# Attention inside a macaron block: one scores pass a round with masks and maxima on VectorE, and probabilities turned by DMA

## The chip, the cores and the metric

The kernel runs on one core of a Trainium2 chip. The metric is the device time of one execution in microseconds. The kernel before took 1144.59 us, the median of three runs (1144.28 to 1146.37).

## The reference

A macaron block on x of shape (8, 256, 256): half a mixture-of-experts FFN, attention, and the same FFN again, each behind a layernorm. Inputs and output are float32.

```python
x = x + 0.5 * ffn(layernorm(x), router_w, gate_w, up_w, down_w)
x = x + attn(layernorm(x), Wq, bq, Wk, bk, Wv, bv, Wo, bo, q_gain)
x = x + 0.5 * ffn(layernorm(x), router_w, gate_w, up_w, down_w)

def attn(x, ...):                      # 16 query heads, 4 key/value heads, head width 16
    q, k, v = x @ Wq.T + bq, x @ Wk.T + bk, x @ Wv.T + bv
    q, k = rope(rms_norm(q)), rope(rms_norm(k))
    q = q * q_gain
    s = where(causal, (q * 16 ** -0.5) @ k.T, -inf)       # 256 x 256 for each head
    return softmax(s) @ v @ Wo.T + bo

def ffn(x, ...):                       # 8 experts, width 512, router weights kept to top-p 0.9
    w = top_p(softmax(x @ router_w.T), 0.9)
    return sum_e w[:, e] * ((silu(x @ gate_w[e].T) * (x @ up_w[e].T)) @ down_w[e].T)
```

## The kernel before

The 2048 tokens lie in 16 tiles of 128, and four tiles are a block. All experts run on all tokens. The FFN work is 64 units (`UNITS`: which FFN, which block, which expert) of four groups each, 256 groups in all. A group is six matmuls of 512 columns into G, six into U (L339, `pe_gu`) and, some slots later, twelve of 256 columns into YB (L358, `pe_y`); products are made of float16 high and low parts, which is why there are so many.

Everything is ordered by hand in slots 0 to 512. `pe_slot`, `act_slot`, `dve_slot`, `pool_slot` and `sp_slot` say what each engine issues in a slot. In an even slot TensorE issues the gate and up matmuls of a group, in an odd slot the down matmuls of an older group, and behind these whatever attention work is due there. Nothing ties an engine to a slot but the order of its own instructions and its waits on semaphores (the lanes in `L`). ScalarE takes the tanh of G (L553) and the high half of the product (L560), VectorE the two products (L685, L690) and the sum into X (L706), GpSimd the low half (L1061). This FFN work runs throughout, for the first FFN and then the second, and attention is threaded between it from about slot 104 to 440.

A batch is two tiles (256 tokens), one even and one odd, and takes 36 slots. Its attention work is:

- `pe_qkv` (L423) makes q, k and v of a tile into S2. VectorE and GpSimd norm and rotate them (the power by -0.5 on GpSimd is L1117). ScalarE (`act_qh`) and VectorE (`dve_ql`) write high and low parts into QS and KS, and SP turns these by transposing DMAs into QKT (`sp_qt`, `sp_kt`).
- The first scores pass, `pe_max` (L443 for even tiles, L449 for odd ones), has queries on partitions and keys along the free axis, into banks S0 and S1: a head pair of 64 contraction rows each, by `tile_position`. VectorE (`dve_max`, L930) adds the mask and takes each row's maximum; `dve_mm` writes it in two parts into spare columns of QS, and `sp_q2` turns the whole of QS a second time.
- The second scores pass, `pe_scores` (L469), runs once for each of 32 items (batch, key/value head), every nine slots. It has keys on partitions and queries along the free axis, in three banks, and the maxima enter the product through the spare rows. ScalarE raises it (`act_exp`, L626), GpSimd zeroes what lies above the diagonal (`pool_mask`, L1149), ScalarE makes the high half (`act_ph`, L634) and GpSimd the low half (`pool_pl`, L1157) in `room`. `pe_pv` (L492) multiplies by v seven slots behind the scores, and VectorE scales the result (`dve_pv`). In this layout the probabilities are already turned as `pe_pv` needs them.
- `pe_op_tp` (L501) and `pe_op_mm` (L507) project the output of a tile, which is added to X.

S2 is shared by `pe_qkv`, `pe_pv`, the output projection and the later routers. A TensorE wait in the middle of this order delays all FFN work behind it.

Of the kernel before, what the change touches and what calls it, by code (L numbers as in the profile page):

```python
# [27 lines left out]
NI = 2 * NT  # L28
# [7 lines left out]
MASKED = -128.0  # L36
# [16 lines left out]
PER = 9  # L53
BATCH = 4 * PER
FIRST = 138
ITEM = [FIRST + PER * i for i in range(NI)]

def by_tile(name):

    first, second, even, odd = AT[name]
    slots = [first, second]
    for t in range(2, NT, 2):
        slots += [FIRST + BATCH * (t // 2 - 2) + even, FIRST + BATCH * (t // 2 - 2) + odd]
    return slots

AT = {'at': (108, 114, 16, 33), 'qkv': (110, 116, 21, 39), 'qt': (117, 123, 28, 46), 'kt': (117, 123, 28, 46), 'q2': (125, 135, 45, 69)}
MAX0 = (120, 122, 126, 128, 130, 132)
MAXB = (38, 41, 50, 56, 59, 66)
OUT = (5, 15)
FTP0 = (3, 3, 6, 6)
FIRST_FTP = (99, 102, 104, 109, 152, 152, 161, 161)
FTP_LATER, ROUTE_LATER = (22, 25)
ROUTE_FIRST = (3, 11, 112, 162)
# [45 lines left out]
def build(nc, d):  # L124
    with ExitStack() as ctx:
# [53 lines left out]
        GM, GE, GR, ESC = (sb(c, [P, 1], F32) for c in ('GM', 'GE', 'GR', 'ESC'))  # L179
# [3 lines left out]
        MB = sb('MB', [P, 2, P], F16)  # L183
# [13 lines left out]
        QS = sb('QS', [P, 2, H, 4, HD], F16)  # L197
# [3 lines left out]
        MXN = sb('MXN', [P, KVH, G // 2, 2], F32)  # L201
        RC = sb('RC', [P, 2 * G], F32)
        RD = sb('RD', [P, 2 * G, HD], F32)
        OB = sb('OB', [P, 2, 2, KVH, G * HD], F32)
# [11 lines left out]
        s_qt, s_q2 = ([sem(f's_{c}{i}') for i in range(2)] for c in ('qt', 'q2'))  # L216
        s_kt = sem('s_kt')
# [4 lines left out]
        for name, labels in [  # L222
# [4 lines left out]
                ('v_fst', 'stats'), ('v_fag', 'aggr'), ('v_fep', 'eps'), ('v_fx', 'xn'), ('v_ls', 'ls mx sub'), ('v_rp', 'sum rc p eq gt'), ('v_wt', 'cum wt'), ('v_wb', 'wtc'), ('v_wc', 'wc'),  # L227
                ('v_al', 'stats aggr eps'), ('v_ax', 'xn'), ('v_qb', 'qb'), ('v_ss', 'ss ms'), ('v_rb', 'rb1 rb0 r'), ('v_qn', 'qn'), ('v_ql', 'qlo klo'), ('v_mp', 'a b'), ('v_mm', 'm1 m2'), ('v_pv', 'rc rd ob'), ('v_op', 'ad'),
                ('g_lo', 'lo'), ('g_w', 'lo2'), ('g_frs', 'rs'), ('g_fl', 'xl'), ('g_rk', 'eq b bp'), ('g_ars', 'rs'), ('g_al', 'xl'), ('g_bo', 'bo'), ('g_sq', 'sq'), ('g_rr', 'rr sg'), ('g_qz', 'z'), ('g_ra', 'ra'), ('g_v', 'v1 r1 v2 r2 v3'), ('g_mk', 'a c'), ('g_pl', 'b a c'), ('g_rw', 'b1 r1 b2 r2 b3')]:
# [62 lines left out]
        def s0_read(eng, s):  # L292
            eng.wait_ge(*L['a_e'].at(before(ITEM, s), 'a'))
            eng.wait_ge(*L['v_mp'].at(before(MAXS, s), 'a'))
# [17 lines left out]
        def s2_read(eng, s):  # L312
            eng.wait_ge(*L['a_e'].at(before(ITEM, s), 'c'))
# [5 lines left out]
            pv_read(eng, s, (3,))  # L319
            if before(ROUTE, s) >= 3:  # L320
                eng.wait_ge(*L['v_ls'].at(before(ROUTE, s), 'ls'))

        def pv_read(eng, s, places):
            i = max((i for i in range(NI) if i % 4 in places and ITEM[i] + I_STEP['pv'] < s), default=-1)
            eng.wait_ge(*L['v_pv'].at(i, 'rd'))
# [79 lines left out]
        def pe_atp(eng, t, s):  # L405
            s1_read(eng, s)
            eng.wait_ge(*L['a_ax'].at(t, 'xh'))
            eng.wait_ge(*L['g_al'].at(t, 'xl'))
            for q in range(2 * KD):
                mm = eng.transpose(S1[:, :].bitcast(F16)[:, q * P:(q + 1) * P], XA16[:, q // KD, q % KD * P:(q % KD + 1) * P], ident16[:, :])  # L410
            mm.then_inc(L['p_at'].sem, 1)

        def pe_qkv(eng, t, s):
# [3 lines left out]
            if t < 2:  # L417
                eng.wait_ge(*L['a_ac'].at(t, 'xt'))
# [8 lines left out]
        def pe_max(eng, n, s):  # L427
            t, j = MAXP[n]
# [4 lines left out]
            if t == 0:  # L433
                eng.wait_ge(s_i2, 3)
            keys = QKT[:, t // 2 % 2, :, H // 2:, :]
            qk = QKT[:, t // 2 % 2, :, :, :]
            rows = lambda h: slice(64 * h, 64 * h + 64)
            if t % 2 == 0:

                for q in range(4):  # L440
                    kv = 2 * j + q // 2
                    for h, bank in ((0, S0), (1, S1)):
                        mm = eng.matmul(bank[:, q * P:(q + 1) * P], qk[rows(h), t % 2, 2 * kv + q % 2, :], keys[rows(h), 0, kv, :], start=q == 0, stop=q == 3, skip_group_check=True, tile_position=(64 * h, 0))  # L443
                        if q == 3:
                            mm.then_inc(L['p_mx'].sem, 1)
# [1008 lines left out]
```

## Time and profile before

| what | value |
|---|---|
| median of three runs | 1144.59 us |
| the profiled execution | 1144.43 us |
| its span, first to last instruction | 1142.2 us |
| TensorE matmuls (PE) | 1112.3 us busy, 97% |
| VectorE (DVE) | 809.9 us busy, 71% |
| GpSimd (POOL) | 668.2 us busy, 59% |
| ScalarE (ACT) | 518.2 us busy, 45% |
| the transposing and loading DMA queue | 11.4% of 16 engines |

Busy time is the time in which an engine had an instruction in work. Matmuls overlap one another, so a group's cost to the span is best read from the starts of its neighbours in the timeline, not from durations. "Idle before" is how long the engine stood idle ahead of a group, and the releaser is what ended that.

### The profile page before, as it was taken

Reading aid. Unit: us, or ns where it says so; the run is one execution under the profiler, and the core shown is the slowest. Engines: PE = TensorE matmul, PEld = TensorE weight load, DVE = VectorE, ACT = ScalarE, POOL = GpSimd, SP = SyncE. Lnnn points to the kernel's source line nnn. Section 1 sums busy time; section 2 is a strip of 40 time slices with the busy share of each in tenths; the row PEclk is TensorE's granted clock in tenths of the full one; section 3 lists DMA queues with packets and bytes.
Section 4 is the critical chain, followed back from the end, with each engine's and each line's share of the span. In section 5 each row is a group of like instructions: output and inputs, shape, how many; then the busy total and the mean of one; then the engine's idle time right before and its main releaser. Section 6 shows DMA issues by size and latency. Waiting matters only on the chain.

```text
span 1142.2 us, 21578 instructions
## 1 busy us (share of the span) xinstructions
PE 1112.3 (97%) x7689; PEld 660.5 (58%) x7689; DVE 809.9 (71%) x1993; ACT 518.2 (45%) x868; POOL 668.2 (59%) x737
## 2 busy tenths in 40 slices
PE   5899999999999999999999999999999999999998
PEld 2456556565555555565565655555656566665665
DVE  7878887679788777778777778768767455554443
ACT  4544544433454554445445454454454544333332
POOL 4545444368488677667767768768655464333222
PEclk9999999999999999999999999999999999999999
DMA  5411110001110110011111011021110000000000
GB/s 185 133 56 56 63 62 2 9 11 42 29 33 15 29 29 19 19 29 24 16 29 24 15 29 24 16 46 25 25 24 20 10 11 1 11 19 1 1 1 20
DMA packets 73273, 34.66 MB, mean 30 GB/s; under 512 B 65360, under 2 KB 69968, under 8 KB 73168
## 3 DMA queue, kind: packets, MB, share of 16 engines
q1 hardware_dynamic: 73168, 33.27, 11.4%
q8 instruction: 64, 1.05, 0.4%
q14 instruction: 41, 0.34, 0.1%
HBM read 15.70 MB, written 2.10 MB: 16 GB/s over the span
## 4 chain that ended last, share of the span: by engine, by line
PE 63%; DVE 5%; POOL 4%; issue 1%; ACT 1%; DVEq 0%; ACTq 0%; POOLq 0%
PE YB L358 19%; PE G L339 19%; PE U L339 18%; PE S L492 1%; PE S L469 1%; PE S L507 1%; DVE S L930 1%; PE S L423 1%; POOL HS L1061 1%; POOL room L1157 1%; DVE TS L685 1%; DVE TS L690 1%; POOL RR L1117 1%; PE S L449 1%; DVE X L706 1%
## 5 line engine op out<-in xcount | busy, mean ns | idle before, releaser
L1061 POOL TENSOR_TENSOR HS<-TS,HS 128x512 f16<-128x512 f32 x256 | 301.1, 1176 | 379.4 <-ACT HS L560 378.4
L358 PE MATMUL YB<-W,HS 128*128 128x256 f16 x3036 | 374.4, 273 | 9.7 <-DVE X L706 6.3
L339 PE MATMUL G<-XS,W 128*128 128x512 f16 x1536 | 375.0, 380 | 1.7 <-ACT XS L585 1.7
L339 PE MATMUL U<-XS,W 128*128 128x512 f16 x1536 | 373.5, 379 | 1.1 <-DVE W L791 1.1
L358 PEld LDWEIGHTS YB<-W,HS 128*128 128x128 f16 x3036 | 290.0, 98 | 92.3 <-DVE X L706 13.4
L685 DVE SCALAR_TENSOR_TENSOR TS<-TS,G 128x512 f32<-128x512 f32 x256 | 175.3, 685 | 223.3 <-ACT TS L553 223.1
L560 ACT ACTIVATE HS<-TS 128x512 f16<-128x512 f32 x256 | 161.4, 631 | 311.7 <-DVE TS L690 311.5
L553 ACT ACTIVATE TS<-G,TSC 128x512 f32<-128x512 f32 x256 | 175.5, 686 | 216.5 <-PE G L339 210.2
L339 PEld LDWEIGHTS U<-XS,W 128*128 128x128 f16 x1536 | 150.3, 98 | 182.9 <-DVE W L791 1.6
L339 PEld LDWEIGHTS G<-XS,W 128*128 128x128 f16 x1536 | 146.9, 98 | 135.3 <-issue 2.0
L690 DVE SCALAR_TENSOR_TENSOR TS<-TS,U 128x512 f32<-128x512 f32 x256 | 176.0, 688 | 28.7 <-DVE TS L685 1.8
L706 DVE SCALAR_TENSOR_TENSOR X<-YB,WTC,X 128x256 f32<-128x256 f32 x253 | 121.9, 482 | 56.0 <-PE YB L358 53.9
L1157 POOL TENSOR_TENSOR room<-room 128x512 f16<-128x512 f32 x96 | 109.9, 1160 | 2.8 <-ACT room L634 2.8
L930 DVE CUSTOM_DVE_ANT_0 S<-S,MB 128x128 f32<-128x128 f32 (+1 forms) x256 | 82.7, 391 | 0.0
L626 ACT ACTIVATE room<-S,ESC 128x512 f32<-128x512 f32 x96 | 62.3, 682 | 16.1 <-PE S L469 15.8
L634 ACT ACTIVATE room<-room 128x512 f16<-128x512 f32 x96 | 59.6, 621 | 17.9 <-POOL room L1149 16.9
L1117 POOL TENSOR_TENSOR RR<-MS,MH 128x20 f32<-128x20 f32 x16 | 56.6, 3540 | 0.2
L1149 POOL TENSOR_SCALAR_AFFINE_SELECT room<-room 128x512 f32<-128x512 f32 x64 | 40.7, 642 | 0.5 <-ACT room L626 0.5
L1070 POOL TENSOR_TENSOR RSF<-VEF,MH 128x1 f32<-128x1 f32 x24 | 14.4, 600 | 42.5 <-DVE VEF L813 42.5
L930 DVE DVE_READ_ACCUMULATOR2_ANT MXN<- 128x1 f32 x256 | 36.3, 142 | 0.0
L492 PEld LDWEIGHTS S<-VS,room 128*128 128x128 f16 x768 | 24.0, 96 | 4.1
L492 PE MATMUL S<-VS,room 128*128 128x49 bf16 x768 | 24.5, 184 | 0.0
(167 smaller groups left out, 712.5 us busy)
## 6 DMA issues: line engine op xcount, KB each, us to landing
room<-in_gate SPq DMA_DIRECT2D x4, 512.0 KB, 3.2
room<-in_up SPq DMA_DIRECT2D x4, 512.0 KB, 3.2
room<-in_down SPq DMA_DIRECT2D x4, 512.0 KB, 3.6
QKT<-in_gate SPq DMA_DIRECT2D x4, 512.0 KB, 3.3
QKT<-in_up SPq DMA_DIRECT2D x4, 512.0 KB, 3.6
QKT<-in_down SPq DMA_DIRECT2D x4, 512.0 KB, 4.5
out_y<-X SPq DMA_DIRECT2D x16, 128.0 KB, 1.8
X<-in_x SPq DMA_DIRECT2D x3, 512.0 KB, 6.2
```

Of the source, the lines that this page charges most:

```text
L339: mm = eng.matmul(bank[:, :], W[:, e, wl, jj, kk * I + m * P:kk * I + (m + 1) * P], flat(XS16[:, b % 2, xl, kk, :, :], 'cq'), start=q == 0 ...
L358: mm = eng.matmul(out, HS[:, j % 2, hl, kk, m * P:(m + 1) * P], W[:, e, wl, 2, kk * D:(kk + 1) * D], start=kk + hl + wl == 0, stop=kk == K ...
L553: eng.activation(TS[:, k % 3, :], GB[k % 2][:, :], ACT.Tanh, scale=TSC[:, e, :]).then_inc(L['a_t'].sem, 1)
L560: eng.activation(HS[:, j % 2, 0, m, :], TS[:, k % 3, :], ACT.Copy).then_inc(L['a_h'].sem, 1)
L626: eng.activation(flat(P32[:, blk, :, :], 'gk'), bank[:, :], ACT.Exp, scale=ESC[:, 0:1]).then_inc(L['a_e'].sem, 1)
L685: eng.scalar_tensor_tensor(TS[:, k % 3, :], TS[:, k % 3, :], 1.0, GB[k % 2][:, :], ALU.add, ALU.mult).then_inc(L['v_t'].sem, 1)
L690: eng.scalar_tensor_tensor(TS[:, k % 3, :], TS[:, k % 3, :], H_C, UB[k % 2][:, :], ALU.mult, ALU.mult).then_inc(L['v_h'].sem, 1)
L706: eng.scalar_tensor_tensor(x, y, WTC[:, b, m, e:e + 1], x, ALU.mult, ALU.add).then_inc(L['v_y'].sem, 1)
L930: mx = eng.tensor_tensor_reduce(x, x, mask, -1.0, 3.0e38, ALU.add, ALU.min, out)
L1061: eng.tensor_tensor(HS[:, j % 2, 1, m, :], TS[:, k % 3, :], HS[:, j % 2, 0, m, :], ALU.subtract).then_inc(L['g_lo'].sem, 1)
L1117: eng.tensor_tensor(RR[:, :], MS[:, :], MH[:, :], ALU.pow).then_inc(L['g_rr'].sem, 1)
L1157: eng.tensor_tensor(flat(PL[:, blk, :, :], 'gk'), flat(P32[:, blk, :, :], 'gk'), flat(PH[:, blk, :, :], 'gk'), ALU.subtract).then_inc(L['g ...
```

## The change

The second scores pass goes, and with it the second turning of QS. There is one pass a round, in the layout of the old `pe_max`, and 48 rounds in place of 32 items: two for each even tile (8 heads each, keys of one tile) and four for each odd tile (4 heads, keys of two tiles), every six slots from slot 128. In a round TensorE fills S0 and S1 (L411 of the new program). VectorE masks, scales by the negative scale and takes the minimum: for even tiles one masking instruction over the bank and one reduction, for odd tiles the old combined instruction twice. ScalarE raises each head by an instruction of its own, with the row's minimum as bias, then makes the high half; GpSimd makes the low half. GpSimd's masking goes. Since probabilities now have queries on partitions, one transposing DMA a round turns high and low parts of both banks (2048 columns, sixteen 128x128 blocks) into QKT or PT1 (`sp_pt`). TensorE waits for that DMA before `pe_pv`, eight slots behind the scores. The transposes of the first two tiles' XA move from TensorE to a DMA. Slots of the projections, the output and the second FFN's normalization shift accordingly.

```diff
-PER = 9
-BATCH = 4 * PER
-FIRST = 138
-ITEM = [FIRST + PER * i for i in range(NI)]
+PER = 6
+BATCH = 6 * PER
+FIRST = 126
+ROUND = [FIRST + 2 + PER * i for i in range(NR)]
+ROUNDS = [(2 * b + (r > 1), r - 2 if r > 1 else r) for b in range(B) for r in range(6)]
...
-Q_STEP = {'rb1': 2, 'sq': 2, 'rb0': 2, 'rr': 3, 'r': 4, 'qn': 5, 'qz': 4, 'v': 5, 'qh': 6, 'ql': 6}
-I_STEP = {'eb': 1, 'ea': 1, 'ma': 2, 'ec': 2, 'hb': 3, 'mc': 3, 'ha': 4, 'lb': 4, 'hc': 5, 'la': 4, 'lc': 5, 'pv': 7, 'o': 8}
+Q_STEP = {'rb1': 2, 'sq': 2, 'rb0': 2, 'rr': 3, 'r': 4, 'qn': 5, 'v': 5, 'qh': 6, 'ql': 6, 't': 7}
+I_STEP = {'ma': 1, 'mb': 2, 'ea': 2, 'eb': 3, 'ha': 3, 'hb': 4, 'la': 4, 'lb': 5, 't': 6, 'pv': 8, 'o': 9}
...
+ATP, QKVP, OUTP = (by_tile(-17, -5), by_tile(-12, 0), by_tile(18, 42))
...
-        def pe_max(eng, n, s):
...
+        def pe_scores(eng, i, s):
+            t, j = ROUNDS[i]
+            s0_read(eng, s)
+            s1_read(eng, s)
+            q_turned(eng, t)
+            k_turned(eng, t)
...
+            heads, keys = (4, 1) if t % 2 == 0 else (2, 2)
+            for q in range(heads):
+                kv, c = (2 * j + q // 2, 4 * j + q) if t % 2 == 0 else (j, 2 * j + q)
+                for h, bank in ((0, S0), (1, S1)):
+                    mm = eng.matmul(bank[:, q * keys * P:(q + 1) * keys * P], QTT[rows(h), t % 2, c, :], KTT[rows(h), t // 2 % 2, 0:keys, kv, :], start=q == 0, stop=q == heads - 1, skip_group_check=True, tile_position=(64 * h, 0))
...
-            part(S2, 1, (1,), 0).then_inc(L['p_s0'].sem, 1)
-            part(S1, 0, (0, 1), 1).then_inc(lane.sem, 1)
-            part(S0, 0, (0, 1), 0).then_inc(lane.sem, 1)
...
+        def pe_pv(eng, i, s):
+            t, j = ROUNDS[i]
             s2_read(eng, s)
+            eng.wait_ge(*L['g_v'].at(t, 'v3'))
+            p_turned(eng, i)
...
+                            mm = eng.matmul(o, PT[i % 2][:, h, hl * G + q * keys + kt, :], VS[:, t // 2 % 3, kt, kv, :], start=kt + hl == 0, stop=kt == keys - 1 and hl == 1)
...
+            for q in range(heads):
+                a = eng.activation(P32[:, h, q * width:(q + 1) * width], (S0, S1)[h][:, q * width:(q + 1) * width], ACT.Exp, bias=MXN[:, i % 2, h, q:q + 1], scale=-1.0)
+            a.then_inc(L['a_e'].sem, 1)
...
+            if t % 2 == 0:
+                x = bank[:, :].rearrange('p (g k) -> p g k', g=G)
+                eng.scalar_tensor_tensor(x, x, NESC[:, 0:1], MB[:, 1, :].unsqueeze(1).broadcast_to([P, G, P]), ALU.mult, ALU.subtract).then_inc(lane.sem, 1)
+                eng.wait_ge(*lane.at(i, 'x' + 'ab'[h]))
+                eng.tensor_reduce(MXN[:, i % 2, h, :], x, AX.X, ALU.min).then_inc(lane.sem, 1)
+            else:
+                for q in range(2):
+                    x = bank[:, q * 2 * P:(q + 1) * 2 * P]
+                    eng.tensor_tensor_reduce(x, x, flat(MB[:, :, :], 'ak'), NESC[:, 0:1], 3.0e38, ALU.add, ALU.min, MXN[:, i % 2, h, q:q + 1]).then_inc(lane.sem, 1)
...
-        def pool_mask(eng, i, c):
...
+        def pool_pl(eng, i, h):
+            eng.wait_ge(*L['a_ph'].at(i, 'ab'[h]))
+            eng.tensor_tensor(PHL[:, i % 2, h, 1, :], P32[:, h, :], PHL[:, i % 2, h, 0, :], ALU.subtract).then_inc(L['g_pl'].sem, 1)
...
-        def sp_q2(eng, t):
...
+        def sp_pt(eng, i):
...
+                eng.wait_ge(*L['p_pv'].at(i - 2, 'pv'))
+            eng.wait_ge(*L['a_ph'].at(i, 'b'))
+            eng.wait_ge(*L['g_pl'].at(i, 'b'))
+            eng.dma_start(PT[i % 2].rearrange('p h c q -> p (h c) q'), flat(PHL[:, i % 2, :, :, :], 'hsk'), transpose=True).then_inc(s_pt[i % 2], 16)
```

TensorE's order in the middle of the attention, before: G, U and YB are the FFN's matmuls, S<-VS,room is `pe_pv`, S<-WO,OT the output projection, and S<-QKT the scores, by L469 in the second pass and by L449 in the first.

```order
L358 MATMUL YB<-W,HS 128x256 x12
L469 MATMUL S<-QKT 128x256
L469 MATMUL S<-QKT 128x512 x2
L469 MATMUL S<-QKT 128x256
L339 MATMUL G<-XS,W 128x512 x6
L339 MATMUL U<-XS,W 128x512 x6
...
L449 MATMUL S<-QKT 128x256 x4
L358 MATMUL YB<-W,HS 128x256 x12
...
L492 MATMUL S<-VS,room 128x49 x24
```

The same engine in the changed kernel, one round of an even tile with the next round's scores: L411 is the scores, L428 `pe_pv` of the round before, from PT1 or QKT.

```order
L411 MATMUL S<-QKT 128x128 x8
L338 MATMUL YB<-W,HS 128x256 x12
...
L428 MATMUL S<-VS,PT 128x49 x16
L338 MATMUL YB<-W,HS 128x256 x12
...
L436 MATMUL S<-ident,OB 128x128 x2
...
L411 MATMUL S<-QKT 128x128 x8
L442 MATMUL S<-WO,OT 128x256 x2
...
L428 MATMUL S<-VS,QKT 128x49 x16
```

The groups of L469 are gone and nothing of their shape has come in; the product with v is in groups of 16 matmuls where it was in groups of 24.

SP's order in one batch before: the last two letters of a name tell what is turned, QS the queries (by L1252 the first time, by L1261 with the maxima), KS the keys, XA the normed tile for the projections.

```order
L1252 DMA_TRANSPOSE QKT<-QS 128x8x128
L1257 DMA_TRANSPOSE QKT<-KS 128x4x128
L1261 DMA_TRANSPOSE QKT<-QS 128x8x128
L1238 DMA_TRANSPOSE XTA<-XA 128x4x128
L1261 DMA_TRANSPOSE QKT<-QS 128x8x128
```

And in the changed kernel, where `room` holds the probabilities (L1164 is `sp_pt`); XS<-XF is for the second FFN.

```order
L1128 DMA_TRANSPOSE XS<-XF 128x4x128 x2
L1134 DMA_TRANSPOSE XTA<-XA 128x4x128
L1147 DMA_TRANSPOSE QKT<-QS 128x8x128
L1155 DMA_TRANSPOSE QKT<-KS 128x4x128
L1164 DMA_TRANSPOSE QKT<-room 128x16x128
L1164 DMA_TRANSPOSE PT<-room 128x16x128
L1147 DMA_TRANSPOSE QKT<-QS 128x8x128
L1155 DMA_TRANSPOSE QKT<-KS 128x4x128
```

The two turnings with maxima have left the queue, and six turnings of sixteen blocks a batch have come in; once a batch one of them stands directly behind those of XA, QS and KS.

## Rows read from the trace of the kernel before

**Rows 1.** The page: busy time and share of the span by engine, then TensorE's granted clock.
```profile
PE 1112.3 (97%) x7689; PEld 660.5 (58%) x7689; DVE 809.9 (71%) x1993; ACT 518.2 (45%) x868; POOL 668.2 (59%) x737
PEclk9999999999999999999999999999999999999999
```

**Rows 2.** Waits of TensorE: us in total, times, longest.
```profile
PE YB L358 <- DVE X L706: 6.3, 8, 1.7
PE YB L358 <- POOL HS L1061: 3.2, 5, 1.9
```

**Rows 3.** The second scores pass among TensorE's groups: busy us, mean ns | idle before.
```profile
L469 PE MATMUL S<-QKT 64*128 64x256 f16 (+1 forms) x128 | 19.8, 330 | 0.0
```

**Rows 4.** TensorE's timeline in the middle of the attention: start us, duration us.
```profile
588.82 1.46 PE L339 MATMUL U<-XS,W 128*128 128x512 f16 x6
590.21 0.39 PE L449 MATMUL S<-QKT 64*128 64x256 f16 x4
590.53 1.49 PE L358 MATMUL YB<-W,HS 128*128 128x256 f16 x12
...
594.66 0.76 PE L492 MATMUL S<-VS,room 128*128 128x49 bf16 x24
595.27 1.47 PE L358 MATMUL YB<-W,HS 128*128 128x256 f16 x12
...
597.44 1.46 PE L339 MATMUL G<-XS,W 128*128 128x512 f16 x6
598.74 1.46 PE L339 MATMUL U<-XS,W 128*128 128x512 f16 x6
600.12 0.62 PE L469 MATMUL S<-QKT 64*128 64x256 f16 x4
600.68 1.48 PE L358 MATMUL YB<-W,HS 128*128 128x256 f16 x12
602.00 1.46 PE L339 MATMUL G<-XS,W 128*128 128x512 f16 x6
```

**Rows 5.** Groups of VectorE, by shape.
```profile
L690 DVE SCALAR_TENSOR_TENSOR TS<-TS,U 128x512 f32<-128x512 f32 x256 | 176.0, 688 | 28.7 <-DVE TS L685 1.8 <-PE G L339 0.5
L948 DVE TENSOR_REDUCE RD<-S 128x128 f32<-128x384 f32 x32 | 16.2, 507 | 0.0
```

**Rows 6.** Groups of ScalarE, by shape.
```profile
L626 ACT ACTIVATE room<-S,ESC 128x512 f32<-128x512 f32 x96 | 62.3, 682 | 16.1 <-PE S L469 15.8
L639 ACT ACTIVATE OT<-S 128x256 f32<-128x256 f32 x16 | 6.0, 376 | 0.0
```

**Rows 7.** Groups of GpSimd, by shape.
```profile
L1061 POOL TENSOR_TENSOR HS<-TS,HS 128x512 f16<-128x512 f32 x256 | 301.1, 1176 | 379.4 <-ACT HS L560 378.4
L1157 POOL TENSOR_TENSOR room<-room 128x512 f16<-128x512 f32 x96 | 109.9, 1160 | 2.8 <-ACT room L634 2.8
L1117 POOL TENSOR_TENSOR RR<-MS,MH 128x20 f32<-128x20 f32 x16 | 56.6, 3540 | 0.2
L1149 POOL TENSOR_SCALAR_AFFINE_SELECT room<-room 128x512 f32<-128x512 f32 x64 | 40.7, 642 | 0.5 <-ACT room L626 0.5
L1112 POOL TENSOR_TENSOR RA<-QKV,COS 128x320 f32<-128x320 f32 x16 | 14.9, 931 | 0.0
```

**Rows 8.** GpSimd's timeline: the first and last of the five instructions of `pool_v`.
```profile
619.07 0.50 POOL L1136 CAST VS<-QKV 128x64 bf16<-128x64 f32 x1
...
620.71 0.24 POOL L1144 CAST VS<-VR 128x64 bf16<-128x64 f32 x1
```

**Rows 9.** DMA issues: count, median us from issue to landing.
```profile
QKT<-QS SPq DMA_TRANSPOSE x32, 2.8
XS<-XF SPq DMA_TRANSPOSE x24, 2.4
```

**Rows 10.** SP's timeline: two turnings issued back to back.
```profile
579.58 1.23 SPq L1252 DMA_TRANSPOSE QKT<-QS  x1
...
580.91 1.22 SPq L1257 DMA_TRANSPOSE QKT<-KS  x1
```

More of the change, by code:

```diff
@@ L52, with by_tile, last_round @@
 PREP = [-99, 0, 8, 24, 36, 47, 58, 72, 83]
-PER = 9
-BATCH = 4 * PER
-FIRST = 138
-ITEM = [FIRST + PER * i for i in range(NI)]
[L61 to L74, printed above, removed]
+PER = 6
[3 more added lines that the diff above has]
+ROUNDS = [(2 * b + (r > 1), r - 2 if r > 1 else r) for b in range(B) for r in range(6)]
+def by_tile(even, odd):
+    return [FIRST + BATCH * (t // 2) + (odd if t % 2 else even) for t in range(NT)]
+def last_round(t):
+    return 6 * (t // 2) + (5 if t % 2 else 1)
 FTP0 = (3, 3, 6, 6)
 FIRST_FTP = (99, 102, 104, 109, 152, 152, 161, 161)
-FTP_LATER, ROUTE_LATER = (22, 25)
-ROUTE_FIRST = (3, 11, 112, 162)
+FTP_SOON, FTP_LATER, FTP_LAST, ROUTE_LATER = ((66, 68), (62, 64), (30, 51), 67)
+ROUTE_FIRST = (3, 11, 112, 174)
 A_STEP = {'ax': 3, 'xl': 3, 'bo': 6}
-Q_STEP = {'rb1': 2, 'sq': 2, 'rb0': 2, 'rr': 3, 'r': 4, 'qn': 5, 'qz': 4, 'v': 5, 'qh': 6, 'ql': 6}
-I_STEP = {'eb': 1, 'ea': 1, 'ma': 2, 'ec': 2, 'hb': 3, 'mc': 3, 'ha': 4, 'lb': 4, 'hc': 5, 'la': 4, 'lc': 5, 'pv': 7, 'o': 8}
+Q_STEP = {'rb1': 2, 'sq': 2, 'rb0': 2, 'rr': 3, 'r': 4, 'qn': 5, 'v': 5, 'qh': 6, 'ql': 6, 't': 7}
+I_STEP = {'ma': 1, 'mb': 2, 'ea': 2, 'eb': 3, 'ha': 3, 'hb': 4, 'la': 4, 'lb': 5, 't': 6, 'pv': 8, 'o': 9}
 R_STEP = {'r1': 1, 'ex': 1, 'r2': 1, 'r2b': 3, 'rank': 3, 'r3': 5}
@@ L215, in build @@
         s_ft, s_at = ([sem(f's_ft{i}') for i in range(2)], sem('s_at'))
-        s_qt, s_q2 = ([sem(f's_{c}{i}') for i in range(2)] for c in ('qt', 'q2'))
-        s_kt = sem('s_kt')
+        s_qt, s_kt = (sem('s_qt'), sem('s_kt'))
+        s_pt = [sem(f's_pt{i}') for i in range(2)]
         N_AW = 8
@@ L403, in pe_ftp @@
             mm.then_inc(L['p_ft'].sem, 1)
[L405 to L411, printed above, removed]
         def pe_qkv(eng, t, s):
@@ L434, in pe_max @@
                 eng.wait_ge(s_i2, 3)
-            keys = QKT[:, t // 2 % 2, :, H // 2:, :]
-            qk = QKT[:, t // 2 % 2, :, :, :]
             rows = lambda h: slice(64 * h, 64 * h + 64)
[L438 to L445, printed above, removed]
-            else:
-                for q in range(2):
-                    for h, bank in ((0, S0), (1, S1)):
-                        mm = eng.matmul(bank[:, q * 2 * P:(q + 1) * 2 * P], qk[rows(h), t % 2, 2 * j + q, :], keys[rows(h), :, j, :], start=q == 0, stop=q == 1, skip_group_check=True, tile_position=(64 * h, 0))
-                        if q == 1:
-                            mm.then_inc(L['p_mx'].sem, 1)
@@ L477, in pe_pv @@
-        def pe_pv(eng, i, s):
-            bank = (S0, S0, S1, S2)[i % 4]
-            (s0_read, s0_read, s1_read, s2_read)[i % 4](eng, s)
-            b, kv = divmod(i, 4)
-            eng.wait_ge(*L['g_v'].at(2 * b + 1, 'v3'))
-            eng.wait_ge(*L['a_ph'].at(i, 'c'))
-            eng.wait_ge(*L['g_pl'].at(i, 'c'))
-            for qt in range(2):
-                for g in range(G):
-                    o = bank[:, (qt * G + g) * VW:(qt * G + g + 1) * VW]
-                    terms = [(g % 2, 2 * qt + g // 2, 0)] + [(2, 2 * (g % 2) + g // 2, 1)] * qt
-                    q = 0
-                    for blk, at, kt in terms:
-                        for ph in (PH, PL):
-                            mm = eng.matmul(o, ph[:, blk, at, :], VS[:, b % 3, kt, kv, :], start=q == 0, stop=q == 2 * len(terms) - 1)
-                            q += 1
+            heads, keys = (4, 1) if t % 2 == 0 else (2, 2)
@@ L1269, in sp_slot @@
+        def sp_slot(eng, s):
+            for i in due(ROUND, s, I_STEP['t']):
+                sp_pt(eng, i)
+            for t in due(ATP, s):
+                sp_atp(eng, t)
+            for t in due(QKVP, s, Q_STEP['t']):
                 sp_qt(eng, t)
-            for t in due(KTP, s):
                 sp_kt(eng, t)
```

286 lines of the change are left out of this document (108 added, 178 removed), and 4 rows, old and new, of the table later.

## The prediction

> **What bounds the kernel now.** I read the page first: TensorE has matmuls in work for 1112.3 of 1142.2 us, no other engine is above 71%, and the granted clock is at its full level (2.4 GHz) in all 40 slices [rows 1]. Then its waits: of those that fall in the steady part the two largest, for VectorE's sum into X and for GpSimd's low half, are 6.3 and 3.2 us together over the whole span [rows 2]. So TensorE is the bound, and the question for each edit is what it does to the stream of matmuls. Durations mislead there, since matmuls overlap; I read the stream by starts [rows 4]. G to U is 1.30 us, YB to the next G 1.32, so a gate, up and down group, two slots, is 3.92 us. Whatever stands between two such starts beyond that is attention's cost on TensorE.
>
> **What goes from TensorE.** The second scores pass: 32 calls of four matmuls. U at 598.74 should be followed by the next group at 600.04; with the call between them YB starts at 600.68, so the call costs 0.64 us, 0.08 of it ahead of its first matmul [rows 4]. The merged busy time of the group, 19.8 us over 32 calls, is 0.62 each, which is the same thing with its tail overlapping what follows [rows 3]. I take 0.65 us: 32 x 0.65 = 20.8 us go. As these stand in the stream of the engine that is the bound, they come off the end in full if nothing new is waited for. The eight small transposes of the first two tiles go too; I leave them out.
>
> At this place a rule can be weighed. The row first: the call streams 2x256 and 2x512 = 1536 columns, with 64 contraction rows in each half of the array. Six full-height matmuls of 512 columns take 1.30 us, 0.42 ns a column, so 1536 columns one after another would be 0.65 us. The call costs 0.64 us [rows 4], so the two halves gain next to nothing here. The Trainium skill (TensorEngine Tiling (Array Packing)) says of contraction dimensions up to 64 that two row tiles work at once, for up to twice the speed. By that the call would be worth 0.32 us and the change 10.4 us instead of 20.8; the trace does not agree.
>
> **What stays the same on TensorE.** The 48 scores calls have the shapes of the old first pass: 16 of eight 128-column matmuls, 32 of four 256-column ones. The old call costs 590.53 - 588.82 - 1.30 = 0.41 us [rows 4], before and after. The product with v is 768 matmuls in both, in 48 calls of 16 for 32 of 24. A call of 24 costs 595.27 - 594.66 = 0.61 us, 25 ns a matmul [rows 4]. If all of that is per matmul, 16 more calls cost nothing; if each has a lead-in like the scores call's 0.09 us (590.21 - 588.82 - 1.30), they cost 1.4 us. I take 0.7.
>
> **The new wait.** TensorE waits for a sixteen-block turning before each `pe_pv`, and all FFN work stands behind it. The trace has no turning of that size. Eight blocks (QS) land 2.8 us after issue, four (XS) 2.4 [rows 9]; a straight line gives 0.1 us a block and 3.6 us for sixteen. From below it is not faster than the four-block one, 2.4; from above twice the eight-block one, 5.6. I take 3.6, as the two rows lie so close together that most of it is fixed. By the Trainium skill (DMA: Bandwidth & Descriptors, on the effective rate of a DMA transpose with a non-contiguous middle dimension, 261 GB/s) the 524 KB would move in an estimated 2.0 us, eight blocks more than QS costing 1.0 and the landing being 3.8; no row here shows that rate by itself.
>
> Is there time for it? Count from the end of a round's scores on TensorE, 0. The matmuls with v come four groups later, with one scores call and one call with v between: 4 x 3.92 + 0.4 + 0.4 = 16.5 us. On the other side:
> - VectorE ends the product with U at about 0.5 and then has an even tile's mask (as L690, 0.69) and the reduction over 512 (L948 has 384 in 0.51, so 0.68) [rows 5]: first bank 1.9. The second bank follows the next sum into X, about 3.8.
> - ScalarE: 256 elements are 376 ns, 512 are 682, so 1.2 ns an element and some 0.22 us for 128, 0.9 us for four heads [rows 6]. Second bank raised by 4.9. S0 and S1 are free then, and the next scores come at 3 x 3.92 + 0.4 = 12.2. That wait is hidden by 7 us.
> - GpSimd has a low half of the FFN at 6.1 to 7.3 (its input comes that late), then the two low halves of the probabilities, 1.16 each [rows 7]: 9.6.
> - The turning is issued at 9.7 and lands at 13.3. Slack 3.2 us.
>
> The tight round is the one in which the next even tile is projected, once a batch for seven batches. GpSimd has squares and rotation (L1112, 0.93) before 0, then the power, 3.54, which can start at about -0.3 and with its small follower ends at 3.6; an FFN low half, 4.8 [rows 7]; the five instructions for v, 620.95 - 619.07 = 1.9 [rows 8], 6.7; another FFN half, 7.9; the low half of the other tile's XA, half the size of L1061, 0.6: 8.5; and the two halves of the probabilities, 10.8. SP has XA, QS and KS ahead of the probabilities in its queue, at 1.33 us from issue to issue [rows 10]: 8.5 + 4.0 = 12.5. Landing at 16.1 against 16.5. The starting points in these two lists are my estimates from the order and these durations, good to about 1 us, so some of the seven rounds will wait: from 0 (all early) to 1.6 us each (the 5.6 landing: 12.5 + 5.6 - 16.5). I take 0.2, 1.4 us in all.
>
> **Other engines.** GpSimd loses 64 maskings of 0.64 us [rows 7] and keeps 96 low halves, in a stream that is off the bound. VectorE keeps the odd tiles' 256-wide instructions, has 0.69 + 0.68 a bank for the even tiles and loses the writing of maxima. ScalarE raises in 256 smaller instructions instead of 96: 128 x 0.22 + 128 x 0.38 = 77 us where it had 96 x 0.68 = 65. It is 45% busy [rows 1], and the tanh it owes TensorE stands behind 0.9 us of this in a slot where it stood behind two of 0.68, so nothing. The lighter VectorE and GpSimd can give back part of the 9.5 us of [rows 2]; bounds 0 and -9.5, and since VectorE's bursts (both banks' maxima in one slot) are spread over two, I take -2.5.
>
> **The sum.** Against the profiled execution's own 1144.43 us (span 1142.2; the median of the runs is 1144.59, the same within 0.2 us): -20.8 + 0.7 + 1.4 - 2.5 = -21.2, which gives 1123.2 us, say 1123.
>
> **Rivals.**
> - A: the tight rounds stall. If sixteen blocks take 5.6 us, seven rounds wait 1.6 us: 11.2 in place of 1.4, 1133. For it: three turnings directly ahead in the queue. Against: the small step from four to eight blocks.
> - B: the bound passes for moments to VectorE or GpSimd in the projection rounds, where the power and both scores' work now meet in six slots instead of nine. At 0.5 us in each of the 16 projection rounds, and nothing given back, that is 8 + 2.5 = 10.5 us more: 1133.7. Against: both engines lose work.
> - C: the second pass was partly hidden, as the rule on row tiles has it, and is worth 10.4 us: 1133.6. Against it the gap in [rows 4].
> - D, slower: the turning becomes the pace of every round. Slack of an ordinary round is 16.5 - 9.7 - landing. With a landing above 6.8 each of 48 rounds waits, and the 21 us are gone at 0.44 us a round, a landing of 7.25. At 8.0: 48 x 1.2 = 58 us, 1181. For it: the probabilities are the longest turning in the kernel, and everything hangs on it. Against: it needs almost three times the eight-block landing.
>
> **How the numbers follow.** A difference of 0.2% (2.3 us) is about what a measurement can tell. Forecast 0.66, between 1118 (all of [rows 2] given back, no stall) and 1128; A 0.14; B 0.08; C 0.04; D 0.05; something between D and A that ends within 0.2% of before 0.03. Faster: 0.66 + 0.14 + 0.08 + 0.04 = 0.92; same 0.03; slower 0.05. The range holds the forecast, A, B and C: 1117 to 1135.
>
> **What the profile after would show.** No group of four matmuls with 512 columns; the scores calls still at 0.41 us and calls with v at 0.40 to 0.49 by starts; TensorE's span less idle down by about 20 us. Sixteen-block turnings landing in 3.6 us. In TensorE's waits, S<-VS waiting for a DMA or its turned probabilities would appear seven times and briefly; many times, or by more than 1 us, is A or D. YB waiting for VectorE or GpSimd for more than the 9.5 us of now is B. A gain near 10 with no such waits is C. The prediction is wrong if the time is above 1135, and its reasoning is wrong if the scores calls have become dearer or the turning lands after 5 us.

## The result, and the profile after

The changed kernel takes 1158.99 us (median; 1156.32 to 1160.62) where the one before, timed beside it, takes 1144.69: a ratio of 1.012 (95% interval 1.0097 to 1.0143). Forecast were 1123.0 us and a range from 1117 to 1135. The change makes the kernel 14 us slower, and the prediction was wrong in sign.

The page of the kernel after, first busy time and share by engine, then TensorE's granted clock in 40 slices:

```profile
PE 1098.6 (95%) x7553; PEld 658.0 (57%) x7553; DVE 834.8 (72%) x1817; ACT 544.0 (47%) x1026; POOL 629.5 (54%) x657
PEclk9999999999999999999999999999999999999999
```

Against [rows 1] TensorE has 13.7 us less in work and its span is 14.2 us longer (1156.4 for 1142.2): the idle time grew by 28 us. No other engine has become the bound. Its waits, in us, times and longest:

```profile
PE YB L338 <- DVE X L627: 16.9, 16, 2.7
PE S L428 <- DMA QKT<-room: 16.3, 8, 3.6
PE YB L338 <- POOL HS L976: 3.8, 5, 0.9
PE S L428 <- DMA PT<-room: 0.7, 1, 0.7
```

Two things stand there that [rows 2] did not have. The product with v (L428) waits for the turning in QKT eight times, in all 16.3 us: once 0.2 us in the first round, and between 1.1 and 3.6 us in each of the seven rounds in which the next even tile is projected, the tight ones of the prediction; and the wait of YB for VectorE's sum into X has gone from 6.3 to 16.9 us. The group of the second pass [rows 3] is gone; what attention has left there is, as line, tile and shape, count, then busy us and mean ns:

```profile
L411 PE MATMUL S<-QKT 64*128 64x128 f16 (+1 forms) x256 | 18.9, 246 | 0.0
L428 PE MATMUL S<-VS,PT 128*128 128x49 bf16 x384 | 13.6, 184 | 0.7 <-DMA PT<-room 0.7
```

Taken by starts, as the prediction did it, one can sum up how much later than usual each group of matmuls starts, given what stands ahead of it. After the first 255 us this excess over the calls' own cost is 7.8 us before and 43.3 after: +35.5. The 32 gaps of the removed pass sum to 20.9. +35.5 - 20.9 = +14.6, against the 14.2 us by which the spans differ. So the account closes with two entries: **the saving came in full, and 35 us of new waits, and of what follows from them, came with it.**

The turnings (count, median us from issue to landing), which answer to [rows 9]:

```profile
QKT<-room SPq DMA_TRANSPOSE x24, 4.3
PT<-room SPq DMA_TRANSPOSE x24, 4.3
QKT<-QS SPq DMA_TRANSPOSE x16, 2.8
QKT<-KS SPq DMA_TRANSPOSE x16, 2.4
```

**A round that waits.** The timeline after, all engines mixed (start us, duration us, engine; in brackets the idle time before and what ended it). It is the tight round of the prediction; its scores end at 684.16.

```profile
683.67 0.32 DVE L812 TENSOR_SCALAR MS<-SS 128x20 f32<-128x20 f32 x1
683.77 0.39 PE L411 MATMUL S<-QKT 64*128 64x256 f16 x4
...
685.70 0.49 DVE L856 CUSTOM_DVE_ANT_0 S<-S,MB,NESC 128x256 f32<-128x256 f32 x1
686.10 0.42 DVE L786 BATCH_NORM_STATS2 STA<-X 128x6 f32<-128x256 f32 x1
...
686.77 0.15 DVE L790 TENSOR_SCALAR VEA<-MVA 128x1 f32<-128x1 f32 x1
...
687.01 0.55 POOL L1003 TENSOR_TENSOR RSA<-VEA,MH 128x1 f32<-128x1 f32 x1 [2.42 <-DVE VEA L790]
...
687.52 3.54 POOL L1032 TENSOR_TENSOR RR<-MS,MH 128x20 f32<-128x20 f32 x1
...
688.43 0.48 DVE L822 TENSOR_TENSOR RA<-RA,RB 128x320 f32<-128x320 f32 x1
...
693.27 1.48 PE L338 MATMUL YB<-W,HS 128*128 128x256 f16 x12 [0.81 <-DVE X L627]
...
696.11 2.27 POOL L1058 TENSOR_TENSOR room<-room 128x512 f16<-128x512 f32 x2
696.24 1.19 SPq L1134 DMA_TRANSPOSE XTA<-XA  x1
...
697.52 1.26 SPq L1147 DMA_TRANSPOSE QKT<-QS  x1
...
698.87 1.22 SPq L1155 DMA_TRANSPOSE QKT<-KS  x1
...
700.20 1.79 SPq L1164 DMA_TRANSPOSE QKT<-room  x1
700.62 1.46 PE L319 MATMUL U<-XS,W 128*128 128x512 f16 x6
...
704.59 0.56 PE L428 MATMUL S<-VS,QKT 128*128 128x49 bf16 x16 [2.52 <-DMA QKT<-room]
```

The power's input MS is there at 683.99, as forecast. But ahead of the power GpSimd has `pool_a_rs` (L1003), the statistic of the odd tile, due in the same slot, and that waits for `dve_a_stats`, which stands in VectorE's order behind the first maxima (L856). GpSimd is idle for 2.42 us and works 0.55 on it; the power starts at +3.4 us where the prediction has -0.3. Everything behind it is late by as much: the low halves of the probabilities end at 698.38, +14.2 (forecast 10.8), and the turning is issued at 700.20, +16.0 (forecast 12.5), behind the three turnings that the prediction counted. It lands 4.3 us later, not 3.6. The product could have started at 701.9. The same wait over the whole span, first after, then before:

```profile
POOL RSA L1003 <- DVE VEA L790: 45.5, 15, 3.6
```
```profile
POOL RSA L1088 <- DVE VEA L869: 13.3, 4, 4.8
```

Eight of the fifteen waits after stand directly ahead of a power, 20.8 us in all; behind the other seven none follows. Two things hang on the late power in this order: the low halves of the probabilities, and the low half of XA (L1007), behind which XA, QS and KS are turned ahead of the probabilities. The halves are ready at +14.2, so 1.8 us of the +16.0 are the queue of SP.

### The profile page after: what moved, and what is told of

Its sections match the earlier page's. It is cut to its first block, busy times and chain, and to the rows that moved or that the text cites. A ratio compares the mean times of both kernels' runs of the same rounds, so it can differ in the third digit from the quotient of the medians.

```text
span 1156.4 us, 21016 instructions
## 1 busy us (share of the span) xinstructions
PE 1098.6 (95%) x7553; PEld 658.0 (57%) x7553; DVE 834.8 (72%) x1817; ACT 544.0 (47%) x1026; POOL 629.5 (54%) x657
## 4 chain that ended last, share of the span: by engine, by line
PE 55%; POOL 8%; issue 3%; DMA 3%; DVE 2%; SPq 1%; ACT 1%; DVEq 0%; POOLq 0%; ACTq 0%
PE YB L338 18%; PE G L319 16%; PE U L319 16%; DMA QKT<-room 3%; POOL RR L1032 2%; POOL HS L976 2%; PE S L442 1%; PE S L428 1%; POOL room L1058 1%; PE S L411 1%; SPq L1155 1%; POOL XF L989 1%; PE S L393 1%; POOL RA L1027 1%; DVE X L627 1%
## 5 line engine op out<-in xcount | busy, mean ns | idle before, releaser
L338 PE MATMUL YB<-W,HS 128*128 128x256 f16 x3036 | 377.3, 274 | 20.8 <-DVE X L627 16.9
L319 PEld LDWEIGHTS G<-XS,W 128*128 128x128 f16 x1536 | 150.0, 98 | 130.8 <-issue 2.6
L551 ACT ACTIVATE room<-S,MXN 128x128 f32<-128x128 f32 (+1 forms) x256 | 90.3, 420 | 28.2 <-DVE MXN L852 15.3
L856 DVE CUSTOM_DVE_ANT_0 S<-S,MB,NESC 128x256 f32<-128x256 f32 x128 | 56.9, 486 | 0.0
L1003 POOL TENSOR_TENSOR RSA<-VEA,MH 128x1 f32<-128x1 f32 x16 | 8.9, 558 | 45.5 <-DVE VEA L790 45.5
L428 PE MATMUL S<-VS,QKT 128*128 128x49 bf16 x384 | 13.7, 184 | 16.3 <-DMA QKT<-room 16.3
L428 PEld LDWEIGHTS S<-VS,QKT 128*128 128x128 f16 x384 | 12.7, 96 | 23.8 <-issue 20.0
L850 DVE SCALAR_TENSOR_TENSOR S<-S,NESC,MB 128x512 f32<-128x512 f32 x32 | 24.0, 751 | 0.0
```

The lines of the kernel that those rows point to most:

```text
L319: mm = eng.matmul(bank[:, :], W[:, e, wl, jj, kk * I + m * P:kk * I + (m + 1) * P], flat(XS16[:, b % 2, xl, kk, :, :], 'cq'), start=q == 0 ...
L338: mm = eng.matmul(out, HS[:, j % 2, hl, kk, m * P:(m + 1) * P], W[:, e, wl, 2, kk * D:(kk + 1) * D], start=kk + hl + wl == 0, stop=kk == K ...
L551: a = eng.activation(P32[:, h, q * width:(q + 1) * width], (S0, S1)[h][:, q * width:(q + 1) * width], ACT.Exp, bias=MXN[:, i % 2, h, q:q + ...
```

## The experiments

Each kernel was timed in three rounds beside the one before (about 1144.3 us there). W is the theory that the place of the odd tile's statistics decides: GpSimd waits for VectorE there, ahead of the power, and the turning is late. Q is its rival, that the turnings' own size and their queue decide, so that an earlier power gives little. All edits but e5's start from the changed kernel.

**e1: the odd tile's norm two slots earlier,** so that its statistics leave the slot of the power.

```diff
-ATP, QKVP, OUTP = (by_tile(-17, -5), by_tile(-12, 0), by_tile(18, 42))
+ATP, QKVP, OUTP = (by_tile(-17, -7), by_tile(-12, 0), by_tile(18, 42))
```

> From the changed kernel (1159.0), the whole normalization of odd tiles, its turning included, two slots earlier. Theory W (wait in front of the power): the changed kernel loses its gain because GpSimd waits in its order for the odd tile's statistics ahead of the 3.5 us power, which then runs 3 to 4 us late and makes the turning of the probabilities, TensorE's wait for it and the late sums into X; so TensorE's waits for turned probabilities fall from 17 us to under 2, those for sums into X from 17 to about 6, the clock stays at full, and the time is 1122 to 1130. Theory Q (queue and size of the turning): the turning is late because it stands behind three others and lands in 4.3 us instead of 3.6; only XA leaves its front, 1.3 of the 2.5 us of each of eight rounds go, and the time is 1146 to 1150.

Measured: 1139.79 us, ratio 0.996 (0.9946 to 0.9975). That is 19.2 us below the changed kernel, by one number in a table. TensorE's waits:

```profile
PE YB L338 <- DVE X L627: 13.6, 24, 2.0
PE S L428 <- DMA QKT<-room: 2.8, 3, 1.6
PE S L428 <- DMA PT<-room: 1.3, 2, 0.7
```

Those for the turning fall from 17.0 to 4.1 us, where W had them under 2, and neither range holds the time: W expected 1122 to 1130, Q 1146 to 1150, and 13.6 us of waits for the sum into X stay where W had about 6. The place of the odd tile's norm matters, and it is not the only cause.

**e2: the odd tile's norm without its turning, two slots earlier.** All that goes by `ATT` moves: the statistics, GpSimd's power for them, and the high and low half of XA. Only the slot in which SP issues the turning of XA stays.

```diff
-ATT = [s - 4 for s in ATP]
+ATT = [s - 4 - 2 * (t % 2) for t, s in enumerate(ATP)]
```

> From the changed kernel, only the statistics and the split of odd tiles two slots earlier; the turning of XA keeps its place behind which the others stand in the queue. Theory W: 1122 to 1132, as the power starts 3 us earlier and all behind it moves. Theory Q: nothing has left the queue, the time stays above 1154.

Measured: 1140.09 us, ratio 0.9963 (0.9948 to 0.9977). The same tight round in e2:

```profile
668.68 0.70 POOL L1003 TENSOR_TENSOR RSA<-VEA,MH 128x1 f32<-128x1 f32 x1 [1.40 <-DVE VEA L790]
...
671.04 0.39 PE L411 MATMUL S<-QKT 64*128 64x256 f16 x4
...
673.92 3.53 POOL L1032 TENSOR_TENSOR RR<-MS,MH 128x20 f32<-128x20 f32 x1
...
679.58 1.19 SPq L1134 DMA_TRANSPOSE XTA<-XA  x1
...
682.38 2.27 POOL L1058 TENSOR_TENSOR room<-room 128x512 f16<-128x512 f32 x2
...
684.75 1.76 SPq L1164 DMA_TRANSPOSE QKT<-room  x1
...
689.16 0.56 PE L428 MATMUL S<-VS,QKT 128*128 128x49 bf16 x16
```

The scores end at 671.43, the turning is issued at +13.3 (it was +16.0), and the product waits for nothing. The edit is worth 18.9 us. The time misses both ranges (W 1122 to 1132, Q above 1154), and the rows show that the edit did not part the two theories. The power starts at +2.5, only 0.9 us earlier than in the changed kernel: GpSimd now waits 1.40 us and works 0.70 for the same statistic ahead of the squares and the rotation, which start 2.1 us later for it. XA is turned at +8.2 where it was +12.1, since its low half no longer stands behind the five instructions for v; so the three turnings are out of the way, and the probabilities go out 0.1 us after their low halves (684.65). Of the 2.7 us, about 1.0 come from GpSimd's earlier halves and 1.7 from the queue. The same holds for e1, where XA is turned at +8.2 in this round too.

**e3: the turning one slot earlier,** ahead of the three others in SP's queue.

```diff
-... 'lb': 5, 't': 6, 'pv': 8, 'o': 9}
+... 'lb': 5, 't': 5, 'pv': 8, 'o': 9}
```

> From the changed kernel, the probabilities' turning is put ahead of XA, QS and KS in the queue, one slot earlier. Theory W: the two low halves are ready 1.8 us before the turning is issued, so at most 1.8 of the 2.5 us of eight rounds go, perhaps with some clock, while the late sums into X stay: 1138 to 1146. Theory Q: all of the wait goes and the sums with it, 1122 to 1130.

Measured: 1143.45 us, ratio 0.9992 (0.9982 to 1.0002), 15.5 us better than the changed kernel; waits for the turning 5.4 us in seven and 0.7 in one, where they were 17.0, those for the sum still 16.9. It lies in W's range (1138 to 1146), not in Q's (1122 to 1130). The power is as late as before (+3.4); the turning goes out at +14.3, right behind the low halves, and the granted clock falls once where it fell three times. The late power and the queue are links of one chain. Taking the queue away alone gives 15.5 us; no run makes the power alone earlier, so its share is not measured by itself.

**e4: the product with v one slot later,** with all that follows it.

```diff
-... 't': 6, 'pv': 8, 'o': 9}
-ATP, QKVP, OUTP = (by_tile(-17, -5), by_tile(-12, 0), by_tile(18, 42))
+... 't': 6, 'pv': 9, 'o': 10}
+ATP, QKVP, OUTP = (by_tile(-17, -5), by_tile(-12, 0), by_tile(19, 43))
```

> From the changed kernel (1159.0), the product with v and its scaling one slot later, the output projection one slot later behind it; GpSimd's order and the queue are untouched. Theory W (the power runs late behind the wait for statistics, and the turning and the sums into X are late with it): the turning is still late, by 2.5 us of which the later place hides 1.3, in eight rounds 10 us, with 3 to 5 us of clock; the late sums into X stay at about 17 us: 1143 to 1148. If instead the turning were the only late thing, the rest of its wait would be small and the time near 1135.

Measured: 1152.83 us, ratio 1.0078 (1.0063 to 1.0093): a miss, 5 us above the expected 1143 to 1148. Waits of TensorE, then two groups and two rows of VectorE and one of GpSimd:

```profile
PE YB L338 <- DVE X L627: 22.6, 22, 2.6
PE S L428 <- DMA QKT<-room: 6.9, 6, 2.0
```
```profile
L869 DVE TENSOR_TENSOR OB<-RD,RC 128x64 f32<-128x64 f32 x32 | 22.4, 700 | 1.1
L869 DVE TENSOR_TENSOR OB<-RD,RC 128x128 f32<-128x128 f32 x16 | 16.1, 1004 | 0.6
```
```profile
574.07 1.08 DVE L869 TENSOR_TENSOR OB<-RD,RC 128x128 f32<-128x128 f32 x1
575.41 0.69 DVE L606 SCALAR_TENSOR_TENSOR TS<-TS,G 128x512 f32<-128x512 f32 x1 [0.27 <-ACT TS L484]
```
```profile
573.84 1.16 POOL L976 TENSOR_TENSOR HS<-TS,HS 128x512 f16<-128x512 f32 x1 [2.28 <-ACT HS L491]
```

The turning's waits fall by 9.4 us, those for the sum rise by 5.7. The small scaling into OB, which takes 345 and 292 ns (128x64 and 128x128, in the mean) in the changed kernel, takes 700 and 1004: 22.7 us more on VectorE. The rows show how: it starts 0.23 us into a low half on GpSimd and ends 0.15 us behind it (575.15 and 575.00).

The Trainium skill (SBUF — State Buffer, Who interferes with whom) says that a VectorE instruction with two SBUF inputs and a GpSimd instruction that reads SBUF contend for a shared pair of ports, and that this pair is an exclusive lock. This row agrees: the scaling ends just behind the low half. It does not hold for every pair here: in the changed kernel VectorE's RA<-RA,RB (L822), also with two SBUF inputs, takes 0.48 us at 688.43 in the middle of GpSimd's power (687.52 to 691.06), and so in all eight rounds in which it falls inside one. That the new waits for the sum come from the longer scaling was not tried by itself. As for the miss, the power starts at +4.4 in the same tight round, 1.0 us later than in the changed kernel, and the turning goes out at +17.1; so the later place hides less than the expectation counted on.

**e5: the removed pass twice.** From the kernel before; each of its 512-column pairs (S1, S0) is issued a second time, to see whether the pass really costs its columns one after another.

```diff
             part(S1, 0, (0, 1), 1)
             part(S0, 0, (0, 1), 0)
+            part(S1, 0, (0, 1), 1)
+            part(S0, 0, (0, 1), 0)
```

> From the kernel before (1144.7), each of the 32 calls of the second scores pass issues its two 512-column matmuls twice. If row tiles do not work at once (the step of the prediction by which the pass is worth 20.8 us), 1024 columns at 0.42 ns are 0.43 us a call and 13.9 us in all: 1158. If they work fully at once, half of that: 1151.6. If the pass was hidden in part, less still.

Measured: 1147.12 us, ratio 1.0024 (1.0013 to 1.0035): +2.7 us on the 1144.41 beside it, where columns one after another would have given 14. It is below the 1151.6 of fully at once, too. TensorE's timeline in e5, start and duration:

```profile
620.02 1.47 PE L358 MATMUL YB<-W,HS 128*128 128x256 f16 x12
621.43 0.71 PE L469 MATMUL S<-QKT 64*128 64x256 f16 x6
622.07 1.47 PE L339 MATMUL G<-XS,W 128*128 128x512 f16 x6
```

622.07 - 620.02 - 1.32 = 0.73 us for the call where [rows 4] have 0.64: 1024 more columns for 0.09 us; one after another they would be 0.43, at once half of that, 0.21. In the kernel before, the weights of this call wait 7.3 us in 32 waits of 0.2 for its first part. The idle time ahead of the call's weight loads falls from 17.5 to 14.4 us in e5, 0.1 us a call, which the doubled pair can hide; so an estimate of its true price is 0.1 to 0.2 us. Two halves of the array do work at once. My reading of the 0.64 us as 1536 columns in series was a coincidence of numbers, and the rule on row tiles that I set aside holds for these columns. The gap of 0.65 that the sum used was read, not derived, and stands.

**e6: e1, e3 and e4 together.**

> From the changed kernel, all three together: odd tiles' normalization two slots earlier, the probabilities' turning first in the queue, the product with v and the output projection one slot later. Theory W: what e1 left, 4 us of waits for turned probabilities, 5 for the output projection's transposes and part of the 14 for sums into X (VectorE's scaling stands in front of a sum there), goes: 1128 to 1134, below both kernels. Rival: TensorE's remaining idle time is VectorE's load, 74% of the span, and moves with it: 1137 to 1140 as in e1.

Measured: 1137.83 us, ratio 0.9945 (0.9928 to 0.9962), in the rival's range. Only one wait for a turning, 0.3 us, is left among TensorE's, yet those for the sum are 17.4 us in 23, and the scaling into OB is as long as in e4. More slack for the turning can then give nothing; most of what remains are waits for VectorE.

**e7: half a turning.** Only the high halves of the probabilities are turned (8 blocks); the low halves are left out of the product, which reads the high ones twice.

```diff
-  eng.dma_start(PT[i % 2].rearrange('p h c q -> p (h c) q'), flat(PHL[:, i % 2, :, :, :], 'hsk'), transpose=True)
+  eng.dma_start(PT[i % 2][:, 0, :, :], flat(PHL[:, i % 2, 0, :, :], 'hk'), transpose=True)
```

> From the changed kernel, only the high halves of the probabilities are turned (eight blocks instead of sixteen) and the product takes them twice; low halves are made but unused, so the result lacks their part. It prices the size of the turning alone. The landing should fall from 4.3 to 2.8 us. Theory W: 1.5 of the 2.5 us of eight rounds go, 12 us and some clock, while the power is as late as before and the sums into X stay: 1140 to 1147. Theory Q (the size and queue are the whole loss): 1122 to 1130.

Measured: 1146.94 us, ratio 1.0028 (1.0016 to 1.004).

```profile
QKT<-room SPq DMA_TRANSPOSE x24, 3.1
```

It lies in W's range (1140 to 1147). The landing falls from 4.3 to 3.1 us and TensorE's waits for it from 16.3 to 9.4, and the time by 12 us. The size matters; but even turnings of eight blocks leave the changed kernel behind the one before, while moving the odd tile's norm at full size does not.

**e8: e6, and VectorE's sum ahead of the first maxima,** by a slot more for the first bank's maxima and its raising.

```diff
-I_STEP = {'ma': 1, 'mb': 2, 'ea': 2, 'eb': 3, ... 't': 5, 'pv': 9, 'o': 10}
+I_STEP = {'ma': 2, 'mb': 2, 'ea': 3, 'eb': 3, ... 't': 5, 'pv': 9, 'o': 10}
```

> From e6 (1137.8), both banks' maxima in the slot after the one in which the first bank's stood, so that VectorE's sum into X, which frees YB for TensorE, comes ahead of them; the raising one slot later for the first bank. Theory W2: what is left is the sum standing behind maxima and attention work in VectorE's order, 17 us of waits in e6; about half goes, 1128 to 1133. Rival L (VectorE's load as such): the sums are late wherever the maxima stand, 1136 to 1140. If the later raising makes the turning late, waits for turned probabilities return and the time is above 1140.

Measured: **1130.81 us**, ratio 0.9882 (0.9868 to 0.9897). In the range of W2, the theory that maxima ahead of the sum make YB wait. This version beats both kernels.

```profile
PE YB L338 <- DVE X L627: 10.6, 12, 2.0
PE YB L338 <- POOL HS L976: 6.1, 6, 1.6
```

**e9: the same without the later product** (e1, the turning at 5, both maxima at 2; `'pv': 8, 'o': 9`, `OUTP` as in the changed kernel).

> As e8, but with the product with v in its old place, eight slots behind the scores (e1 with the turning first in the queue and the maxima behind the sum). Against e8 it prices the later product. Theory W2: 1130 to 1136, as some turnings have no slack left. Rival L: 1138 to 1142.

Measured: 1137.99 us, ratio 0.9946 (0.9929 to 0.9963), 2 us above W2's range (1130 to 1136) and at the lower end of the rival's: 11.9 us of waits for the sum, 3.3 for a turning. The later product is worth 7.2 us here and 6.2 in e4. Without it the new order gives little: e9 is only 1.8 us below e1.

**e10: e8 with the odd tile's norm late again** (`by_tile(-17, -5)`).

> From e8 (1130.8), only the odd tiles' normalization put back two slots later, where the changed kernel has it. Theory W: the power starts 3 us late again behind the wait for the statistics; the later product hides part of the turning's lateness, the rest and the late sums return, 7 to 14 us: 1138 to 1145. If the order of the statistics were only worth something together with the changed kernel's tight product, it would be within 2 us of e8.

Measured: 1135.26 us, ratio 0.9925 (0.9905 to 0.9945): 4.5 us lost, not the expected 7 to 14. GpSimd still waits ahead of the power:

```profile
672.29 0.55 POOL L1003 TENSOR_TENSOR RSA<-VEA,MH 128x1 f32<-128x1 f32 x1 [1.61 <-DVE VEA L790]
672.80 3.54 POOL L1032 TENSOR_TENSOR RR<-MS,MH 128x20 f32<-128x20 f32 x1
```

but products wait for a turning only once, 0.3 us. The price of the late norm is not the length of the wait on GpSimd; it is 19 us where the turning has no slack and 4.5 where it has.

## Why the prediction was wrong

- **The pass that goes, 20.8 us: right.** The gaps sum to 20.9. That it was read from starts and not from the columns made it robust: by e5 the explanation beside it was wrong, and rival C did not come all the same. The rule speaks of the columns, and 1536 of them in two halves at once would be 0.32 of the call's 0.64 us; what the rest is, no run shows.
- **Lead-in of more product calls, 0.7 us: about right.** A call of 16 costs 0.41 us by starts, in sum about 0.2 us more than before.
- **The tight round: this step failed.** The prediction lists what GpSimd has before the turning as squares and rotation "before 0, then the power, 3.54, which can start at about -0.3". The list leaves out `pool_a_rs`, which the order has in front of the power in that very slot, with a wait on VectorE. From -0.3 to +3.4 is a shift of 3.7 us, 3.5 of them left at the issue, and the list behind it is otherwise right to a tenth or two (low halves +14.2 for 10.8 + 3.5, issue +16.0 for 12.5 + 3.5). At 12.5 even the true landing of 4.3 would have come at 16.8, against 17.8 when the product was in fact due (a wait of 0.81 us for the sum and a call of the router, L370, with 0.4 us had moved it from 16.5). So in this round the landing alone brings no wait. e2 bears that out: issued at +13.3, a turning of 4.3 us holds up nothing. Rival A had the kind and the place of the wait right, in just the seven rounds counted, and priced it at 11 us for a long landing; its cause was another. How much of the 19 us the wait costs through the power and how much through XA's late turning in the queue is open; both hang on it in the changed kernel.
- **The landing, 3.6 us: too small, within the bounds.** 4.3. The straight line through four and eight blocks gave 0.1 us a block; sixteen lie 0.19 a block above eight. Its issue takes 1.8 us of SP's queue, too, where the small ones take 1.2. Half a turning gives 12 us back (e7), in rounds that were already late.
- **Recovered waits, -2.5 us: wrong sign.** The lighter VectorE does not wait less: it was not lighter (834.8 for 809.9 us busy), and YB's waits for its sum rose by 10.6. The prediction put the first maxima ahead of the sum and looked only at what this does to the scores banks, not at who waits for the sum; e8 against e6 gives 7 us for that order with the later product; with the product in its old place the new order, together with the earlier turning, gives 1.8 (e9 against e1), so it is not shown that the order causes the 10.6 in the changed kernel. This is rival B, with VectorE as its engine: it had 8 us of new waits.
- **ScalarE, 77 us for the raising: too small.** 90.3. The instruction with a bias takes 369 ns for 128 elements and 472 for 256, where the straight line had 220 and 380; no wait of TensorE is put down to it.
- **The lower bound:** the prediction puts 1118 for "all of [rows 2] given back, no stall". Its own terms give 1144.4 - 20.8 + 0.7 - 9.5 = 1114.8, so the range should have begun lower. The result does not turn on it.

In these terms the 35.5 us are: 19 in the calls with v (38.9 us in the stream where 48 at 0.41 are 19.7), 10.6 at the sum, and 6 spread over the rest. Some of it, in the 19 too, is the clock's. Three times the granted clock fell behind such a wait; TensorE's timeline and the window from 362 to 366 us (us, busy time and count of PE, PEld, DVE, ACT and POOL, then the granted clock, 0.58, and the DMA share and GB/s):

```profile
361.67 0.64 PE L428 MATMUL S<-VS,QKT 128*128 128x49 bf16 x16 [2.75 <-DMA QKT<-room]
362.13 2.74 PE L338 MATMUL YB<-W,HS 128*128 128x256 f16 x12
364.66 1.82 PE L319 MATMUL G<-XS,W 128*128 128x512 f16 x6
```
```profile
362.00:366.00 4.00, 4.00 (x26) 2.52 (x23) 1.37 (x4) 0.48 (x1) 3.38 (x3) 0.58 0.16 33
```

After 2.75 us of waiting the engine ran at its lower level (1.2 GHz), and twelve matmuls that take 1.31 us by starts took 2.53.

**What stays open.** e8 is still 8 us above the forecast, with 16.7 us of waits of YB. VectorE's share in them can come from instructions made long by GpSimd's and from its order; which of the two weighs more was not tried. The length alone does not set them: in e9 the scalings into OB are short again (293 ns for 128x128) and the sum is waited for 11.9 us, in e8 they are long (961 ns) and it is 10.6. The wait in the head of the attention (the first rounds, from 304 us) was not separated from the tight rounds either.

## What to carry to other kernels

When a step hands work from engine to engine, list what is due on each of them in that slot from the order itself, waits included; here a small instruction with a wait stood ahead of a long one, and moving the work that it belongs to by two slots, one number in a table, gave back 19 us. Then ask it again for every engine whose instruction was moved ahead of another: who waits for the one that now comes second. The tight round had 0.4 us of slack in a count of 16.5: price such slack as if gone, and expect one missed wait to be paid once a batch.

## What the hardware showed

- A turning of sixteen blocks lands in 4.3 us and one of eight, half its data, in 3.1 (2.8 for QS); four take 2.4.
- 1024 more columns in two half arrays cost 0.09 us by starts, 0.1 to 0.2 by the estimate under e5, where 0.43 would be serial.
- VectorE's scaling of 128x128 with two SBUF inputs takes 292 ns in the changed kernel and 1004 in the mean in e4, where it meets GpSimd's low halves and ends right behind them. The low half of the keys (128x128, two SBUF inputs, L836) went from 314 to 787 ns in the mean with the change itself: 0.34 us at 693.92, and 1.24 at 722.62, where it meets a low half of the probabilities. Inside GpSimd's power neither L822 (0.48 us) nor the scaling (0.23 us at 690.67) was longer.
